# Set-up of a graph and mixture-of-experts kernel reordered: adjacency first, no low parts on GpSimd

## The reference

```python
x0 = layernorm(x)
h = x0 @ fc_w.T + fc_b
w_eff = (w * clip(d, 0, 1)) @ w.T
for _ in range(8):
    f = sigmoid(alpha) * 0.5 * (adj @ h - h) + h @ w_eff - h + x0
    h = h + f / 8
x = x + h
t = layernorm(x)
# 8 experts, the best 2 of each token by softmax(t @ router_w.T), weights renormalised
out = x + t + sum_e combine[:, e] * (gelu(t @ w1[e] + b1[e]) @ w2[e] + b2[e])
```

## Time and profile before

| | |
|---|---|
| Runs | 566.61, 569.12 and 1095.98 us, median 569.12 |
| Profiled execution | 567.61 us, its span 565.8 us |
| Busy | TensorE 546.7 us (97%), VectorE 435.5 (77%), ScalarE 307.3 (54%), GpSimd 61.3 (11%) |
| Chain that ended last | TensorE 91%, VectorE 5%, ScalarE 2%, DMA 1% |
| Set-up | up to 57.88 us, where the first tile of Q starts |
| Iteration 0 | 57.88 to about 95 us |

### The profile page before, as it was taken

One profiled execution on the slowest core, in us unless ns is written; L12 is line 12 of the kernel. 1 busy time (PEld: TensorE's weight loads), 2 busy tenths in 40 slices (PEclk: granted clock), 3 DMA queues, 4 the chain that ended last, 5 costly groups with the idle time before them and its releaser, 6 DMA issues.

```text
span 565.8 us, 9264 instructions
## 1 busy us (share of the span) xinstructions
PE 546.7 (97%) x3023; PEld 474.5 (84%) x3023; DVE 435.5 (77%) x1104; ACT 307.3 (54%) x530; POOL 61.3 (11%) x45
## 2 busy tenths in 40 slices
PE   2999999999999999999999999999999999999797
PEld 2777997997899788987899788987899788987585
DVE  5889776679766995679766995589766994489695
ACT  4432333558535783458435783468445772158484
POOL 2320102101020101100110101110110101010100
PEclk9999999999999999999999999999999999999899
DMA  6100010072004501062104501162104400160151
GB/s 198 38 1 0 1 39 2 6 242 90 20 18 149 186 0 37 17 244 75 31 6 151 185 2 35 27 240 69 38 2 148 148 17 21 47 241 13 41 186 39
DMA packets 25759, 43.15 MB, mean 76 GB/s; under 512 B 1462, under 2 KB 20236, under 8 KB 23820
## 3 DMA queue, kind: packets, MB, share of 16 engines
q1 hardware_dynamic: 25740, 42.91, 22.6%
HBM read 38.45 MB, written 4.46 MB: 76 GB/s over the span
## 4 chain that ended last, share of the span: by engine, by line
PE 91%; DVE 5%; ACT 2%; issue 1%; DMA 1%; SPq 0%; DVEq 0%; ACTq 0%
PE bank L938 28%; PE bank L940 27%; PE bank L939 27%; PE bank L1064 2%; DVE scs L541 1%; PE bank L957 1%; PE bank L1084 1%; DVE work L808 1%; PE bank L1078 1%; DMA work<-in_adj_dram 1%; PE bank L1071 1%; PE bank L1119 1%; PE bank L1093 1%; ACT work L413 0%; PE bank L966 0%
## 5 line engine op out<-in xcount | busy, mean ns | idle before, releaser
L475 ACT ACTIVATE work<-bank,cols 128x512 f32<-128x512 f32 x128 | 87.0, 680 | 17.9 <-PE bank L940 17.8
L371 ACT ACTIVATE scs<-work 128x512 fp32r<-128x512 f32 (+1 forms) x129 | 82.8, 642 | 25.0 <-DVE work L808 24.1
L541 DVE TENSOR_TENSOR scs<-work,scs 128x512 fp32r<-128x512 f32 x128 | 87.0, 679 | 1.4
L938 PE MATMUL bank<-M,GT 128*128 128x384 f32 x192 | 65.7, 342 | 0.0
L940 PE MATMUL bank<-M,GT 128*128 128x384 f32 x192 | 65.0, 339 | 0.0
L939 PE MATMUL bank<-M,GT 128*128 128x384 f32 x192 | 65.0, 339 | 0.0
L808 DVE TENSOR_TENSOR work<-work,GT 128x512 f32<-128x512 f32 x90 | 60.8, 680 | 2.6 <-ACT work L475 2.1
L541 DVE TENSOR_TENSOR GT<-bank,GT 128x512 fp32r<-128x512 f32 x48 | 32.2, 687 | 37.8 <-ACT GT L371 37.6
L867 DVE TENSOR_TENSOR Q<-bank,bias 128x384 f32<-128x384 f32 x64 | 35.6, 557 | 32.7 <-PE bank L940 31.7
L371 ACT ACTIVATE GT<-bank 128x512 fp32r<-128x512 f32 x48 | 27.6, 593 | 58.5 <-PE bank L940 56.0
L334 POOL TENSOR_TENSOR rstd<-ve,nhalf 128x8 f32<-128x8 f32 x16 | 29.5, 1844 | 267.7 <-DVE ve L559 267.7
(11 more groups left out here) (182 smaller groups left out, 1281.2 us busy)
## 6 DMA issues: line engine op xcount, KB each, us to landing
GT<-comb_rows SPq DMA_DIRECT2D x8, 1536.0 KB, 7.0
Q<-comb_rows SPq DMA_DIRECT2D x16, 512.0 KB, 6.5
GT<-comb_rows SPq DMA_DIRECT2D x7, 1024.0 KB, 6.3
xn<-in_x_dram SPq DMA_DIRECT2D x16, 256.0 KB, 7.8
out_dram<-outs SPq DMA_DIRECT2D x16, 256.0 KB, 2.3
GT<-comb_rows SPq DMA_DIRECT2D x7, 512.0 KB, 4.3
work<-in_adj_dram SPq DMA_DIRECT2D x4, 256.0 KB, 5.2
Q<-in_L_ffn_w_dram SPq DMA_DIRECT2D x2, 512.0 KB, 5.7
```

The lines of the kernel that those rows point to most:

```text
L371: return nc.scalar.activation(dst, src, ACT.Copy)
L475: nc.scalar.activation(hid[:, i % 2, :], bank[UP_BANK[i % 3]][:, :], ACT.Gelu, bias=cols[:, B1_COL + e:B1_COL + e + 1]).then_inc(gelu_done, 1)
L541: return v.tensor_tensor(dst, src, hi.bitcast(FP32), ALU.subtract)
L938: pe.matmul(dst, wh, xh, start=start, stop=False)
```

## The change

The DMAs of adj go ahead of x; w1 and w2 are loaded later, over the adjacency in `work`, behind a new semaphore (lnat_summed). TensorE makes the four tiles of L^2 right after L's transposes, with the powers of R between them, and then the products with x0. The low parts of Lns, w1 and w2 move from GpSimd to VectorE, tile by tile for Lns; those of w1 and w2 stand in the first iteration's Q loop (i = 1 and 3). ScalarE makes the high parts of Lns tile by tile between the scalings. VectorE makes the statistics of x(0) after the weights' transposes instead of first, the statistics of x(1) in the set-up, the row sums of L tile by tile, and the split of b2 (split_b2) in the first iteration before scale_z. power_tile(2, 0) goes ahead of the feature powers. In iteration 0 the transposes of z use banks 7 and 6 instead of 7 and 3, and both stand directly after nodes_product(1).

```diff
@@ -120,6 +119,7 @@
         Lnat = work[:, 0:4]
+        w12_raw = work[:, 0:4].rearrange("p (k r) n -> p k (r n)", k=2).rearrange("p k (e c) -> p k e c", c=D)
@@ -258,7 +260,6 @@
-            load_x(0)
@@ -266,9 +267,8 @@
                 sp.dma_start(rows[k - NT:k - NT + E, :], src).then_inc(rows_in, 16)
+            load_x(0)
             sp.dma_start(w_raw[:, 1, :], fc_w).then_inc(fc_in, 16)
-            sp.dma_start(w12_raw[:, 0], w1.rearrange("e c f -> c e f")).then_inc(w12_in, 16)
-            sp.dma_start(w12_raw[:, 1], w2.rearrange("e f c -> f e c")).then_inc(w12_in, 16)
@@ -304,6 +304,9 @@
             next_x(1)
+            sp.wait_ge(lnat_summed, 1)
+            sp.dma_start(w12_raw[:, 0], w1.rearrange("e c f -> c e f")).then_inc(w12_in, 16)
+            sp.dma_start(w12_raw[:, 1], w2.rearrange("e f c -> f e c")).then_inc(w12_in, 16)
@@ -343,13 +346,6 @@
             inverse_root(0, 0)
-            pool.wait_ge(lnat_hi, 1)
-            nc.gpsimd.tensor_tensor(Lns[:, 1], Lnat, Lns[:, 0].bitcast(FP32), ALU.subtract).then_inc(lnat_lo, 1)
-            for k in range(2):
-                pool.wait_ge(wsp_hi, k + 1)
-                nc.gpsimd.tensor_tensor((w1s, w2s)[k][:, 1], w12_raw[:, k],
-                                        (w1s, w2s)[k][:, 0].bitcast(FP32), ALU.subtract).then_inc(wsp_lo, 1)
@@ -407,29 +403,36 @@
+            def high_natural(t):
+                act.wait_ge(lnat_ready, t + 1)
+                high(Lns[:, 0, t], Lnat[:, t, :]).then_inc(lnat_hi, 1)
...
                                      scale=node[:, 3, t:t + 1]).then_inc(adj_scaled, 1)
-            high_lt(0, [0])
+                if t >= 1:
+                    high_natural(t - 1)
+            high_natural(NT - 1)
+            high_lt(0)
+            high_lt(1, range(NT - 1))
             high_x0(0)
-            high_lt(0, range(1, NT))
-            act.wait_ge(lnat_ready, NT)
-            high(Lns[:, 0], Lnat).then_inc(lnat_hi, 1)
+            high_lt(1, [NT - 1])
...
             high_x0t(0, X0_SETUP)
-            high_lt(1)
-            act.wait_ge(w12_in, 32)
-            high(w1s[:, 0], w12_raw[:, 0]).then_inc(wsp_hi, 1)
-            high(w2s[:, 0], w12_raw[:, 1]).then_inc(wsp_hi, 1)
+            high_lt(2, [0])
...
             high(M[:, 0], SK.rearrange("p (j i) c -> p j i c", i=BABY)).then_inc(m_hi, 1)
-            high_lt(2)
+            high_lt(2, [1])
+            act.wait_ge(w12_in, 32)
+            for k in range(2):
+                high((w1s, w2s)[k][:, 0], w12_raw[:, k]).then_inc(wsp_hi, 1)
+                high_lt(2, [2 + k])
@@ -622,9 +627,6 @@
             step(v.tensor_scalar(node[:, 0, :], node[:, 2, :], -DT * 0.5, 1.0 - DT, ALU.mult, ALU.add))
-            for b in range(GB):
-                norm_x_stats(0, b)
-            ln_var(0, 0)
@@ -634,15 +636,16 @@
+            def low_natural(t):
+                dve.wait_ge(lnat_hi, t + 1)
+                low(Lns[:, 1, t], Lnat[:, t, :], Lns[:, 0, t]).then_inc(lnat_lo, 1)
...
                 diagonal(t)
-            v.tensor_copy(pick[:, :], ident[0:GB * V, 0:C])
-            scale_first_x0()
-            low_lt(0, [0])
-            for b in range(GB):
-                low_x0(0, b)
-                low_lt(0, [b + 1])
-            low_lt(0, range(GB + 1, NT))
+                if t >= 1:
+                    low_natural(t - 1)
+            low_natural(NT - 1)
+            low_lt(0)
@@ -650,18 +653,26 @@
             v.tensor_scalar(wT[:, 1, :], bank[1][:, 0:P], dclip[:, :], None, ALU.mult).then_inc(wt_ready, 1)
+            for b in range(GB):
+                norm_x_stats(0, b)
+            ln_var(0, 0)
+            dve.wait_ge(weff_mm, 1)
+            v.tensor_scalar(Rp[:, 0, :], bank[1][:, P:2 * P], DT, None, ALU.mult).then_inc(pow_ready, 1)
+            low_lt(1, [0])
...
             v.tensor_scalar(ones[:, :], ident[:, :], 0.0, 1.0, ALU.mult, ALU.add).then_inc(ones_ready, 1)
-            dve.wait_ge(weff_mm, 1)
-            v.tensor_scalar(Rp[:, 0, :], bank[1][:, P:2 * P], DT, None, ALU.mult).then_inc(pow_ready, 1)
-            low_gt(0, 0, 0)
-            low_gt(0, 2, 1)
+            scale_first_x0()
             power_out(1, 2, 1, bank[3])
+            low_lt(1, [1])
+            for t in range(2):
+                v.tensor_reduce(node[:, 4, t:t + 1], Lnat[:, t, :], AX.X, ALU.add)
+            power_out(2, 3, 2, bank[3])
             for b in range(GB):
-                low_x0t(0, b, X0_SETUP)
-            step(v.tensor_reduce(node[:, 4, :], Lnat, AX.X, ALU.add))
-            power_out(2, 3, 2, bank[3])
-            low_lt(1, [0])
+                low_x0(0, b)
+            low_lt(1, [2])
+            for t in range(2, NT):
+                last = v.tensor_reduce(node[:, 4, t:t + 1], Lnat[:, t, :], AX.X, ALU.add)
+            last.then_inc(lnat_summed, 1)
@@ -672,30 +683,30 @@
-            dve.wait_ge(pow_ready, 4)
-            sum_powers(1)
-            low_lt(1, [1])
-            sum_powers(2)
-            low_lt(1, [2])
...
-            for c in range(BABY):
+            def evacuate_crep(c):
...
                 last.then_inc(crep_ready, 1)
-            sum_powers(3)
...
+            dve.wait_ge(pow_ready, 4)
+            sum_powers(1)
             low_lt(1, [3])
-            for i in range(4, STEPS):
+            sum_powers(2)
+            low_gt(0, 0, 0)
+            low_gt(0, 2, 1)
+            for c in range(BABY):
+                evacuate_crep(c)
+            for b in range(GB):
+                low_x0t(0, b, X0_SETUP)
+            for i in range(3, STEPS):
                 sum_powers(i)
+            v.tensor_copy(pick[:, :], ident[0:GB * V, 0:C])
@@ -709,12 +720,16 @@
                 last.then_inc(m_sum, 1)
-                if c > 0:
+                if c == 0:
+                    low_lt(2, [0])
+                else:
                     low_gt(0, 2 * c - 1, 1 + c)
+            for b in range(GB):
+                norm_x_stats(1, b)
+            ln_var(0, 1)
...
             low(M[:, 1], SK.rearrange("p (j i) c -> p j i c", i=BABY), M[:, 0]).then_inc(m_lo, 1)
-            low_lt(2, [0])
...
+            low_lt(2, [1])
@@ -725,14 +740,27 @@
             dve.wait_ge(crep_ready, BABY)
+            dve.wait_ge(lnat_summed, 1)
...
             step(v.tensor_reduce(node[:, 5, :], v2_diag, AX.X, ALU.add))
+            low_lt(2, [2])
             bias_term(2)
-            low_lt(2, range(1, NT))
+            low_lt(2, [3])
...
+            def low_weights(k):
+                dve.wait_ge(wsp_hi, k + 1)
+                low((w1s, w2s)[k][:, 1], w12_raw[:, k], (w1s, w2s)[k][:, 0])
...
+            def split_b2():
+                dve.wait_ge(b2_in, 16 * 4 * GB)
+                step(v.tensor_copy(b2_high.bitcast(F32R), b2_raw[:, 1]))
+                step(v.tensor_tensor(b2_high, b2_raw[:, 1], b2_high, ALU.subtract))
+                step(v.tensor_copy(b2s[:, :, :], b2_raw[:, 0]))
+                v.tensor_tensor(b2s[:, :, :], b2s[:, :, :].bitcast(FP32), b2_high, ALU.add).then_inc(small_ready, 1)
@@ -867,7 +893,9 @@
                         route_on(g - 1, 2 + i)
-                    if not final and i == 2:
+                    if first and i in (1, 3):
+                        low_weights(i // 2)
+                    if not first and not final and i == 2:
@@ -910,13 +938,14 @@
                         low_x0t(g + 1, b)
+                    split_b2()
...
                     for b in range(GB):
-                        low_z(g, b)
+                        low_z(g, b, ZT_FIRST)
@@ -969,6 +998,8 @@
                 for t in range(NT):
+                    if k == 1 and a == 0:
+                        pe.wait_ge(lt_lo, t + 1)
@@ -983,37 +1014,35 @@
                         last.then_inc(lt_mm, 1)
-            pe.wait_ge(x0_lo, 1)
-            for t in range(NT):
-                pe.wait_ge(lt_lo, t + 1)
-                nodes_product_tile(0, t)
...
             pe.transpose(bank[1][:, 0:P], w_raw[:, 0, :], ident[:, :]).then_inc(w_t, 1)
-            pe.wait_ge(x0_lo, GB)
-            nodes_product(2)
+            pe.wait_ge(lnat_lo, NT)
+            power_tile(1, 0)
...
             pe.matmul(bank[1][:, P:2 * P], wT[:, 1, :], wT[:, 0, :], start=True, stop=True).then_inc(weff_mm, 1)
+            power_tile(1, 1)
+            pe.wait_ge(pow_ready, 1)
+            pe.matmul(bank[3][:, 0:P], Rp[:, 0, :], Rp[:, 0, :], start=True, stop=True).then_inc(pow_mm, 1)
+            power_tile(1, 2)
+            pe.wait_ge(pow_ready, 2)
+            pe.matmul(bank[3][:, 0:2 * P], Rp[:, 1, :], Rp[:, 0:2, :], start=True, stop=True).then_inc(pow_mm, 1)
+            power_tile(1, 3)
+            pe.wait_ge(pow_ready, 3)
+            pe.matmul(bank[1][:, :], Rp[:, 3, :], Rp[:, 0:4, :], start=True, stop=True).then_inc(pow_mm, 1)
+            pe.wait_ge(x0_lo, GB)
+            nodes_product(0)
+            nodes_product(2)
+            pe.wait_ge(lt_lo, 2 * NT)
...
                 times_powers(bank[CREP_BANK[c]], cols[:, FB_COL:FB_COL + 1].to_broadcast([P, P]), c).then_inc(crep_mm, 1)
```

(71 more changed lines are left out.)

16 lines of the change are left out of this document (removed).

## The result

The changed kernel takes 562.15 us (median of 6 runs, 560.41 to 562.87), the kernel before 566.79 (median of six, 566.37 to 569.12 and the 1095.98). Runs in a disturbed, slow state, like the 1095.98, are left out of every ratio. The ratio is 0.9894, 95% interval 0.9869 to 0.9919: 6.0 us, between 4.6 and 7.4. The two medians differ by 4.6 us, the low end of this. In a second session it was 560.78 us with a ratio of 0.988 [0.9847, 0.9912]. The two profiled executions differ by 6.1 us of span, 565.8 against 559.7.

What follows compares the result with a forecast made beforehand. TensorE, busy 97% of the span, was taken as the bound. Q moves from 57.88 to 54.8 (gain 3.1), with the first iteration's 0.9 a gain of 4.0; 567.6 - 4.0 = 563.6, predicted as 563.5, range 561.7 to 566.3.

Steps and rivals of the forecast that it cites:

- the argument about VectorE: Set-up: VectorE takes 5.2 us of low parts from GpSimd, but 7.0 us of stretching beside GpSimd's big tensors goes.
- split_b2 in front of scale_z: First iteration: split_b2 (1.5 us) now precedes scale_z, where VectorE waits 0.55; z's second half comes 0.9 later, at 88.8.
- z's bank: First iteration: z's second transposition gets bank 6, ending a 1.0 us wait; gain counted 0.9, from 0.4 to 1.0.
- Rival (a): Loads: issue order does not bring the adjacency forward, tiles arrive from 7.3; gain 2.0, time 565.6; chance 0.11.
- (c): Set-up: x arrives late and becomes the bound; landing from 18.9 on loses the gain, at 21 gives 569.7; chance 0.03.
- (d): Set-up: VectorE remains stretched although GpSimd's low parts are gone; time 565.1; chance 0.06.
- if the place alone counts, and 5.0 if the tiles follow each other: Loads: bounds for the second adjacency tile's arrival, 6.3 by place in the issue order, 5.0 by 0.7 to 0.9 spacing.
- the 11.5 that I took: Set-up: start of TensorE's squaring, taken between 10.8 and 12.1, 5.8 us after the second adjacency tile.
- the 54.8 of the sum: End of set-up: Q's start after the change, 11.5 + 42.6 + 0.7, against 57.88 before, a gain of 3.1.
- The idle at 38.41: TensorE before Q in the kernel before: one idle of 0.2 us, part of 1.0 idle between 14.01 and 57.88.
- The hole at the powers: Set-up: TensorE waits 0.7 us at the second product of powers for VectorE's power_out(1, 2, 1), 6.9 against 6.2.
- Rival (b): Set-up: thin transposes between 5 and 11.5 bring TensorE's clock down, costing 2 us; gain 2.0, time 565.6; chance 0.07.

Runs made afterwards that it cites:

- z_bank_back: The changed kernel with z's second transposition in bank 3 again, behind the low part of the product there: 562.45 us, ratio 0.9894.
- gpsimd_busy: The changed kernel with two unused 128x1024 additions on GpSimd, started when the low parts of x0's transposes are there: 562.59 us, ratio 0.9902.
- before_vector_lows: The kernel before with only the low parts of Lns, w1 and w2 made by VectorE: 567.28 us, ratio 0.999.
- power_first: The changed kernel with VectorE's power_out(1, 2, 1) in front of scale_first_x0: 563.26 us, ratio 0.9918.
- changed_again: The changed kernel, unedited, measured once more in a second session: 560.78 us, ratio 0.988.

## Why the prediction was right in kind and wrong in size

**The steps that held.** Most of the gain is at TensorE's start, and the pieces summed for it had the right sizes: 5.8 us from the second adjacency tile to the squaring, measured 5.7 from the 4.7 at which it is scaled. Both halves of the argument about VectorE were right: the long L653 and L670 were GpSimd's doing, and were hidden. split_b2 in front of scale_z cost nothing, and z's bank gave 0.9 (1.2 by z_bank_back). The loads of w1 and w2, m_sum and v2_read were never waited for. Rival (a) falls, (c) falls (the statistics at 12.83 wait for nothing), (d) falls by gpsimd_busy.

**The term that failed: "if the place alone counts, and 5.0 if the tiles follow each other".** Both ends for the second tile were too late. It was there by 4.7, when the second scaling begins, and the third at 5.96, where I had let x's second half (6.30) speak for the second place. The 6.30 was that of one execution: in before_vector_lows, with the same loads, the eight statistics run as one piece from 4.20. The start came 1.1 us before the 11.5 that I took, and 0.4 before the earlier end.

The tile was the wrong one as well. ScalarE's last wait in this stretch is for the third. The changed kernel once more:

```profile
6.20 0.72 ACT L413 ACTIVATE work<-work,node 128x512 f32<-128x512 f32 x1 [0.24 <-DMA work<-in_adj_dram]
```

The squaring starts 4.45 us after this scaling, at 10.65. In the changed kernel, z_bank_back, gpsimd_busy and power_first, whose edits do not touch the start, it is 4.44 to 4.45 too, and the start is at 10.39 to 10.81. So 0.4 us of it is chance, and 10.41 is a lucky one.

Of the 2.2 us by which Q came before the 54.8 of the sum, this term is 1.1 us. The next two paragraphs have 0.2 for the idle time and 0.3 for the hole, and some 0.6 stay open.

**The idle at 38.41.** I wrote 0.2 us, from the bracket of the row. By the starts of the pieces it is 0.6: the same two feature products that begin at 36.77 take 1.0 us in the changed kernel, where nothing waits behind them, and the next pass stood 1.64 later. This is 0.4 us of gain overlooked, and it works against the holes before 16.21, which by the same reading are 0.6 together and not 0.8.

**The hole at the powers** was 0.36 us and not 0.7: VectorE's chain took 6.6 us from wt_ready at 12.9, not 6.9, and TensorE, with more in front of it, was itself at w_eff only at 13.25. The sum with the measured values: 3.6 for the start, 0.6 and 0.6 for the idle that went, 0.3 for the small transposes, less 0.4 for the hole, is 4.7 of the 5.3 up to Q. The last 0.6 is spread over first passes after a wait (0.34 instead of 0.23 each) and 0.14 at x0's transposes; I did not resolve it further. With z's 0.9 the 5.3 are the 6.2 at the logits. The low end of the forecast gain is added up wrongly: 57.88 less 12.1, 42.6 and 1.0 is 2.2, with 0.4 it is 2.6 and not 2.7.

**"A measurement of this kernel tells about 2% from no change."** That sentence was wrong by a factor of eight: the interval is 0.25% wide to each side, so a forecast of 0.7% was one of a measurable gain and should have been called so.

**The clock.** I had taken the printed 1.00 as evidence that TensorE runs fast from the first slice, and set the Trainium skill against it (TensorE: Matmul & The Clock Gate, Part 1, a clock that starts low and rises with activity). The durations of the transposes agree with that page, 421 ns in the median in all ten profiles against 272 once the clock is up, and the printed 1.00 was no measurement there. Rival (b) had the price about right (2 us; 1.5 to 1.6 between profiles) and its place, but it is no cost of the change: the kernels in the old order pay it too, in before_vector_lows for twelve passes from 14.71 on. It moves the profiled set-up by chance; in the totals it was not told apart.

## What to carry to other kernels

Before a load is moved forward, look for what stands at the front of each queue behind the load that is moved back: the same edit moved TensorE's start forward by 3.7 us in one order of the work and back by 2.4 in the other. Read idle time and clock from the starts of equal instructions, not from the printed bracket or clock. Where TensorE's dense stretch is short or waits stand before it, compare executions in which the passes have the same pace, or keep the engine busy in both.

## What the runs showed of the hardware that I had not expected

- TensorE's clock is low at the program's start (128x128 transposes of 421 ns; four of them in 1.07 us, and in 0.60 a microsecond later) while the profile prints 1.00 for want of a record. In seven of ten profiles it was still or again low in the dense stretch; with eleven small products before it, in none of three. Three of the ten were fast without them, so three may be chance in part.
- Between GpSimd and VectorE the one that is stretched changes. Beside 128x1024 additions on GpSimd, fifteen VectorE instructions went from 3.61 to 8.00 us. Beside VectorE's low part of M (128x1152), GpSimd's root of 128x8 went from 1.67 to 2.69. VectorE's low parts from PSUM and its statistics did not change (2.48 and 1.64).
- The granted clock in the drain fell to 0.50 for some 3 to 4 us in some executions, for a cost of 1.5 us. In the changed kernel's profile it fell just behind 2.2 us in which TensorE waited, but changed_again has the same order of work and no fall. The mean clock was 0.999 or 1.000 in all six runs of z_bank_back and of gpsimd_busy, which differ from the changed kernel only in the first 90 us, and below that in six of the changed kernel's twelve. What decides it stays open.
